# Moving part of the weight quantisation from the attention stage into the V projection, with smaller reduction pieces and a third x3w buffer

## The chip, the cores and the metric

The kernel runs on the 8 cores of one Trainium2 chip. Each core takes one of the 8 batch rows, 2048 tokens of width 1024, and runs the same program; no core talks to another. The metric is the device time of the slowest core in microseconds, as the median over runs.

## The reference, cut to what matters

```python
x = x + _layernorm(_L0_attn_ref(_layernorm(x), wq, bq, wk, bk, wv, bv, wo, bo))
x = x + _layernorm(_L0_ffn_ref(_layernorm(x), w1, conv_w, conv_b, w2))

def _L0_attn_ref(...):        # 16 heads of 64, blocks of 128 queries
    ...
    scores = jnp.einsum('bhnqd,bhnkd->bhnqk', qb, kb) / float(np.sqrt(D))
    scores = jnp.where(band, scores, -jnp.inf)      # each block sees itself and its two neighbours
    ...

def weight_quant(w):
    scale = 1.0 / jnp.clip(jnp.mean(jnp.abs(w)), 1e-05)
    return jnp.clip(jnp.round(w * scale), -1, 1) / scale

def _L0_ffn_ref(x, w1, conv_w, conv_b, w2):
    ...
    h = bit_linear(x, w1)                 # activations to 8 bits, weights to -1, 0, 1
    h = depthwise_conv1d(h.transpose(0, 2, 1), conv_w, conv_b)
    h = h.transpose(0, 2, 1)
    h = jax.nn.silu(h)
    return bit_linear(h, w2)
```

Both feed-forward weights (1024 x 4096, 16.8 MB each as float32) must be read twice: once for the mean of their absolute values, and once to be rounded to -1, 0 or 1 with the scale that comes from that mean.

## The kernel before

The program is a list of blocks. Inside a block each engine (SP, TensorE or PE, VectorE or DVE, ScalarE or ACT, GpSimd or POOL) replays its own list in the order in which the Python code called `p.op`; it waits on semaphores where the call says so. Nothing reorders an engine's list. At the end of a block each engine waits for its own semaphores, its DMAs among them, and all engines meet at a barrier.

- **b1** (to 107 us): layer norm of x and its transposition into `B1`.
- **b2** (107 to 393 us): the projections. GpSimd's queue loads `wq` and `wk` (16 DMAs, float32 in memory, written as bf16, 256 KB each on arrival), later `wv` (8 DMAs, issued when the Q projection is through). SP's queue loads the feed-forward weights in pieces into two buffers `wstage` (L324), and DVE sums their absolute values (L326): 16 pieces of `w1t`, 128 x 2048 (1 MB), then 32 pieces of `w2t`, 128 x 1024 (512 KB). A piece is loaded when the piece before last has been summed. PE meanwhile does the Q and K projections (L339). When the last sum is there, a few small steps give the scales `swc` (L359 to L376, the last one named `n6`); then DVE takes the maxima of Q and K (L387, L390), a chain of small steps gives the softmax bound, with one small DMA on SP's queue (L407), and the V projection follows: 32 groups of 8 matmuls (L439) in four PSUM slots, each moved out by DVE (L445).
- **b3** (393 to 887 us): the attention, 16 heads of 18 key blocks, 288 iterations, 256 of them with work on all engines: scores on PE (L582), exponential on ACT (L589), mask on POOL (L595), three matmuls of the result (L553), reciprocal and scaling on DVE (L561, L563). After each iteration `tern_gen` is asked for two steps of the weight quantisation. It works through 64 jobs of 128 x 1024 in pairs, 10 steps a pair: two loads (L488), two `tern_u` (L494, called n1 here), two more passes in place (L501, n2), two last passes (L510, n3) and two stores (L518). With a and b for the two slots of a pair, the order is La Lb n1a n1b n2a n2b n3a n3b Sa Sb. There are two slots, so the load of a slot waits until the store of the pair before has landed. 32 pairs take 160 iterations; the last 128 iterations have none. Jobs 0 to 31 are `w1t` (stored as int8 in `w1i`), jobs 32 to 63 are `w2t` (bf16, `w2b`).
- **b4** (887 to 1209 us): output projection, layer norms, 8-bit quantisation of the activations into `x3tsp`.
- **b5** (1209 us to the end): the feed-forward part in 8 stages of 256 tokens. Stage s does, chunk by chunk (32 chunks), the convolution of s (L927) and the first matmul of s + 2 (L898, on `w1h` from GpSimd's queue, L880, and `x3w` from SP's queue, L870), and then the second matmul of s - 1 (L967, `w2b` by SP, L952). `x3w` has two buffers. Its load stands at the head of a stage in SP's list, behind the two output stores (L1005) of the second matmul before:

```python
    for s in range(NS):
        s2 = s + 2
        if s2 <= NS:
            emit_x3ld(s2)
        for hcx in range(HCH):
            emit_conv_chunk(s, hcx)
```

Of the kernel before, what the change touches and what calls it, by code (L numbers as in the profile page):

```python
# [6 lines left out]
F32 = mybir.dt.float32  # L7
BF16 = mybir.dt.bfloat16
# [11 lines left out]
D = 1024  # L20
# [84 lines left out]
def build_nc():  # L105
# [68 lines left out]
    bks = alloc("bks", [128, NC], F32)  # L174
    bvrow = alloc("bvrow", [1, D], F32, side="right")
    borow = alloc("borow", [1, D], F32, side="right")
    bvB = alloc("bvB", [128, D], F32, side="right")
    boB = alloc("boB", [128, D], F32, side="right")
# [117 lines left out]
    free("xin_0", "xin_1", "x1b_0", "x1b_1", "ptr_0", "ptr_1", "pbc_0", "pbc_1")  # L296

    wsb = [[alloc(f"wsb{s}_{c}", [128, D], BF16) for c in range(NC)] for s in range(2)]
    wstage = [alloc(f"wstage_{i}", [128, 2048], F32) for i in range(2)]
# [3 lines left out]
    p = Plan()  # L303
    wq_ld = [0] * NC
# [54 lines left out]
    n1 = p.op("tensor", lambda e: e.matmul(pms[0:1, 0:48], onescol[:, :], wsum[:, 0:48],  # L359
                                           start=True, stop=True),  # L360
              waits=[(sV, red_done[-1])], inc=sT)
    n2 = p.op("scalar", lambda e: e.copy(mrow[0:1, 0:48], pms[0:1, 0:48]),
              waits=[(sT, n1)], inc=sS)
    p.op("vector", lambda e: e.reduce_sum(mtot[0:1, 0:1], mrow[0:1, 0:16], axis=AXX),
         waits=[(sS, n2)])
    nr2 = p.op("vector", lambda e: e.reduce_sum(mtot[0:1, 1:2], mrow[0:1, 16:48], axis=AXX))
# [61 lines left out]
    for t in range(NT):  # L428
        for ofs in range(2):
# [8 lines left out]
            for ic in range(NC):  # L438
# [11 lines left out]
                waits=[(sT, last)], inc=sV)  # L450

# [16 lines left out]
    tern_jobs = []  # L468
    for ch in range(NC):
        for q in range(4):  # L470
            tern_jobs.append((dw1t[ch * 128:(ch + 1) * 128, q * 1024:(q + 1) * 1024],
                              dw1i[q, :, ch * 1024:(ch + 1) * 1024], 0))
    for ch in range(HCH):
        tern_jobs.append((dw2t[ch * 128:(ch + 1) * 128, :],
                          dw2b[:, ch * 1024:(ch + 1) * 1024], 1))
    tstate = {"sp": [0, 0]}

    def tern_steps():
        for i0 in range(0, len(tern_jobs), 2):
            picks = [k for k in (i0, i0 + 1) if k < len(tern_jobs)]  # L480
            lds, n1s, n2s, obufs = {}, {}, {}, {}
            for k in picks:
                srcA, dst, wi = tern_jobs[k]
                slot = k % 2
                wl = [(sV, n6)]
                if tstate["sp"][slot]:
                    wl.append((sSp[slot], tstate["sp"][slot]))
                lds[k] = p.op("sync", lambda e, srcA=srcA, slot=slot: e.dma_start(  # L488
                    out=wstage3[slot][:, :], in_=srcA), waits=wl, inc=sW[slot], amt=16)
                yield  # L490
            for k in picks:
                wi = tern_jobs[k][2]
                slot = k % 2
                n1s[k] = p.op("vector", lambda e, slot=slot, wi=wi: e.tensor_scalar(  # L494
                    out=tern_u16[slot][:, :], in0=wstage3[slot][:, :],
                    scalar1=swc[:, wi:wi + 1], scalar2=RC, op0=ALU.mult, op1=ALU.add),
                    waits=[(sW[slot], lds[k])])
                yield
            for k in picks:
                slot = k % 2  # L500
                n2s[k] = p.op("vector", lambda e, slot=slot: e.tensor_scalar(  # L501
                    out=wstage3[slot][:, :], in0=tern_u16[slot][:, :],
                    scalar1=RD, scalar2=1.0, op0=ALU.subtract, op1=ALU.min),
                    waits=[(sV, n1s[k])])
                yield
            for k in picks:
                slot = k % 2
                wi = tern_jobs[k][2]
                obufs[k] = tern8[slot] if wi == 0 else tern2b[slot]
                n2s[k] = p.op("vector", lambda e, slot=slot, obuf=obufs[k]: e.tensor_scalar(  # L510
                    out=obuf[:, :], in0=wstage3[slot][:, :],
                    scalar1=-1.0, scalar2=None, op0=ALU.max),
                    waits=[(sV, n2s[k])], inc=sV)
                yield
            for k in picks:
                slot = k % 2
                dst = tern_jobs[k][1]
                tstate["sp"][slot] = p.op("sync", lambda e, dst=dst, slot=slot, obuf=obufs[k]: e.dma_start(  # L518
                    out=dst, in_=obuf[:, :]), waits=[(sV, n2s[k])], inc=sSp[slot], amt=16)
                yield  # L520

    tern_gen = tern_steps()

    def win(j):
        q0 = (j - 1) * 128
        q1 = (j + 2) * 128
        c0 = max(0, -q0)
# [488 lines left out]
    for s in range(NS):  # L1016
        s2 = s + 2
        if s2 <= NS:
            emit_x3ld(s2)
# [165 lines left out]
```

How the kernel before makes its waits and increments, by code:

```python
    def replay(self, eng, e, hwm):  # L60
        for w, emit, inc, amt in self.items[eng]:
            for s, v in w:
                if hwm[eng].get(s.name, 0) < v:
                    e.wait_ge(s.h, v)
                    hwm[eng][s.name] = v
            ins = emit(e)
            if inc is not None:
                ins.then_inc(inc.h, amt)
        for s in self.incs[eng].values():
            if hwm[eng].get(s.name, 0) < s.n:
                e.wait_ge(s.h, s.n)
                hwm[eng][s.name] = s.n
```

## Time and profile before

| | us |
|---|---|
| median of 2 runs | 2260.27 (2257.5 and 2263.03) |
| the profiled execution | 2256.83 |
| span of its slowest core, core 1 | 2255.3 |
| spans of the other cores | 2236.7 to 2248.0 |
| busy in that span: PE, DVE, ACT, POOL | 1216.7, 975.6, 619.8, 321.6 |

No engine is busy for much more than half of the span, so the time is made of stages with different limits, one behind the other. All rows below are of core 1 of the profiled execution; times in a timeline run from the start of its span.

### The profile page before, as it was taken

How to read it: one execution, taken by the hardware profiler on the slowest of the kernel's cores; microseconds unless marked ns; L12 is line 12 of the kernel's file. 1: busy time of each engine (PE TensorE's matmuls, PEld its weight loads, DVE VectorE, ACT ScalarE, POOL GpSimd, SP SyncE). 2: the span in 40 equal slices, each digit the busy share in tenths (PEclk: the TensorE clock that was granted, in tenths of full speed). 3: DMA queues.
4: the chain of work that ended last, by engine and by line, in shares of the span. 5: the costliest groups of instructions: out<-in, count | busy, mean ns of one | idle time of the engine just before them, and what ended most of it. 6: DMA issues, size and time to landing. Idle time of an engine off the chain costs nothing. (4 is left out here: it accounts for less than half of the span.)

```text
span 2255.3 us, 24795 instructions; the slowest of 8 cores (2236.7 to 2255.3 us)
## 1 busy us (share of the span) xinstructions
PE 1216.7 (54%) x6594; PEld 627.6 (28%) x6594; DVE 975.6 (43%) x2260; ACT 619.8 (27%) x1648; POOL 321.6 (14%) x383
## 2 busy tenths in 40 slices
PE   2349519232333475444441767757676757655455
PEld 1124204111111132111110555525252525242122
DVE  3434473454555543555551004535252525262624
ACT  2314200221222354122220345515151615141200
POOL 0000000333333487000000111101010101000000
PEclk9999759555555555666665888889898989858588
DMA  2398600333344202222225785646464646454044
GB/s 70 100 247 222 195 28 1 112 99 111 126 137 139 99 1 48 41 56 59 54 59 116 177 224 132 150 179 157 173 163 158 178 167 170 141 149 144 33 134 174
DMA packets 155324, 277.63 MB, mean 123 GB/s; under 512 B 27827, under 2 KB 114100, under 8 KB 144822
## 3 DMA queue, kind: packets, MB, share of 16 engines
q1 hardware_dynamic: 72966, 184.68, 25.6%
q0 software_dynamic: 82224, 91.37, 18.2%
q8 instruction: 59, 0.97, 0.2%
q14 instruction: 75, 0.61, 0.1%
HBM read 220.57 MB, written 29.36 MB: 111 GB/s over the span
## 5 line engine op out<-in xcount | busy, mean ns | idle before, releaser
L898 PE MATMUL pA<-x3w,w1h 128*128 128x256 bf16 (+1 forms) x2304 | 289.2, 273 | 96.8 <-DMA w1h<-w1i 75.5
L595 POOL TENSOR_TENSOR expm<-expraw,sb_mask 128x384 bf16<-128x384 bf16 (+1 forms) x256 | 231.2, 918 | 450.0 <-ACT expraw L589 380.1
L967 PE MATMUL pM<-w2b,H2q 128*128 128x512 bf16 x1024 | 250.8, 404 | 67.6 <-DMA w2b<-w2b 44.1
L898 PEld LDWEIGHTS pA<-x3w,w1h 128*128 128x128 bf16 x2304 | 218.8, 103 | 147.0 <-issue 107.3
L553 PE MATMUL pod<-VA,expm 128*128 128x65 bf16 x768 | 103.3, 228 | 289.4 <-DVE B L563 155.5
L1031 DVE TENSOR_REDUCE apar<-H 128x256 f32<-128x2048 f32 x32 | 116.7, 3650 | 313.7 <-ACT H L933 313.7
L589 ACT ACTIVATE expraw<-psc,negC 128x384 bf16<-128x384 f32 (+1 forms) x256 | 145.0, 568 | 344.0 <-PE psc L582 321.2
L927 PE MATMUL pC<-Ab,diag 128*128 128x256 bf16 x768 | 149.4, 311 | 137.9 <-DVE tland L1101 83.4
L909 ACT ACTIVATE Ab<-pA,mwc 128x256 bf16<-128x256 f32 (+1 forms) x288 | 129.6, 450 | 147.0 <-PE pA L898 141.7
L880 POOL DMA_DIRECT2D w1h<-w1i x72 | 63.0, 875 | 733.8 <-PE pA L898 448.2
L553 PEld LDWEIGHTS pod<-VA,expm 128*128 128x128 bf16 x768 | 58.1, 107 | 388.7 <-issue 387.4
L967 PEld LDWEIGHTS pM<-w2b,H2q 128*128 128x128 bf16 x1024 | 101.6, 103 | 217.8 <-issue 121.5
L985 DVE BATCH_NORM_STATS2 stat<-out 128x6 f32<-128x512 f32 x16 | 11.0, 690 | 313.2 <-ACT out L981 313.2
L933 ACT ACTIVATE H<-pC,cbs 128x256 f32<-128x256 f32 x256 | 120.5, 471 | 60.5 <-PE pC L927 59.2
L339 PE MATMUL pq<-B,wsb 128*128 128x512 bf16 x512 | 112.5, 383 | 34.6 <-DMA wsb<-wq 34.6
L326 DVE TENSOR_REDUCE wsum<-wstage 128x1 f32<-128x1024 f32 (+1 forms) x48 | 75.5, 1575 | 111.9 <-DMA wstage<-w2t 58.1
L582 PE MATMUL psc<-QT,KT 64*128 64x384 bf16 (+1 forms) x256 | 123.0, 481 | 1.5 <-PEq L83 1.3
L494 DVE TENSOR_SCALAR tern_u<-wstage,swc 128x1024 int16<-128x1024 f32 x64 | 50.9, 797 | 168.5 <-DMA wstage<-w1t 91.7
L927 PEld LDWEIGHTS pC<-Ab,diag 128*128 128x128 bf16 x768 | 65.1, 104 | 200.7 <-issue 191.0
L981 ACT ACTIVATE out<-pM,sc2b 128x512 f32<-128x512 f32 x32 | 20.1, 679 | 305.8 <-PE pM L967 305.8
L682 PE MATMUL po<-wo,B 128*128 128x512 bf16 x256 | 90.3, 529 | 23.5 <-DMA wo<-wo 14.3
L1101 DVE TENSOR_TENSOR tland<-H,sxB 128x256 f32<-128x256 f32 x256 | 96.9, 419 | 4.4 <-ACT sxB L1089 3.2
(134 smaller groups left out, 1304.1 us busy)
## 6 DMA issues: line engine op xcount, KB each, us to landing
w1h<-w1i POOLq DMA_DIRECT2D x72, 1024.0 KB, 5.7
w2b<-w2b SPq DMA_DIRECT2D x64, 1024.0 KB, 5.2
wstage<-w2t SPq DMA_DIRECT2D x64, 512.0 KB, 4.1
wstage<-w1t SPq DMA_DIRECT2D x16, 1024.0 KB, 8.3
wstage<-w1t SPq DMA_DIRECT2D x32, 512.0 KB, 5.2
xin<-x SPq DMA_DIRECT2D x16, 512.0 KB, 3.7
w2b<-tern2b SPq DMA_DIRECT2D x32, 256.0 KB, 2.0
xre<-x SPq DMA_DIRECT2D x16, 512.0 KB, 5.8
```

What stands on the lines that cost most here:

```text
L339: last = p.op("tensor", lambda e, oc=oc, st=st, ic=ic, slot=slot, wset=wset: e.matmul(pq[slot][:, :], wsb[wset][ic][:, oc * 128:(oc + 1) * ...
L553: last_use = p.op("tensor", lambda e, qb=qb, j=j, h=h, sl=sl, wc=wc, first=first, lastc=lastc: e.matmul(pod[qb % 4][:, 0:65], expm[sl][:, ...
L582: nmm = p.op("tensor", lambda e, hc=hc, hr=hr, j=j, sl=sl, q0r=q0r, q1r=q1r, c0=c0, c1=c1: e.matmul(psc[sl][:, c0:c1], KT[hc][hr:hr + 64, ...
L589: psc_ev[sl] = p.op("scalar", lambda e, h=h, sl=sl, c0=c0, c1=c1: e.activation(out=expraw[sl][:, c0:c1], in_=psc[sl][:, c0:c1], func=AF.Ex ...
L595: mask_done[sl] = p.op("gpsimd", lambda e, sl=sl, c0=c0, c1=c1: e.tensor_tensor(expm[sl][:, c0:c1], expraw[sl][:, c0:c1], mask01[:, c0:c1] ...
L898: last = p.op("tensor", lambda e, j=j, hs2=hs2, d=d, slotp=slotp, mv=mv, width=width: e.matmul(pA[slotp][:, 0:width], w1h[j % 2][:, d * 51 ...
L909: pa_ev[slotp] = p.op("scalar", lambda e, s2=s2, hcx=hcx, slotp=slotp, width=width: e.activation(out=ab(s2, hcx)[:, 0:width], in_=pA[slotp ...
L927: last = p.op("tensor", lambda e, s=s, hcx=hcx, k=k: e.matmul(pC[:, 0:256], dg(k, hcx), ab(s, hcx)[:, k:k + 256], start=(k == 0), stop=(k ...
L933: silu_d[s][hcx] = p.op("scalar", lambda e, s=s, hcx=hcx: e.activation(out=H2[:, hcx * 256:(hcx + 1) * 256], in_=pC[:, 0:256], func=AF.Sil ...
L967: last = p.op("tensor", lambda e, sm=sm, hcx=hcx, tsl=tsl, ofs=ofs, b=b, qq=qq, slot=slot: e.matmul(pM[slot][:, :], H2q[sm % 2][:, hcx * 2 ...
L1031: apar_d[s][g3] = p.op("vector", lambda e, g3=g3: e.reduce_max(apar[:, g3 * 256:(g3 + 1) * 256], H2.ap().rearrange("p (c n) -> p n c", c=H ...
L1101: ntl[i] = p.op("vector", lambda e, hcx=hcx, i=i: e.tensor_tensor(tland[i][:, :], H2[:, hcx * 256:(hcx + 1) * 256], sxB[:, :], ALU.mult), ...
```

## The change

Four things change.

1. The quantisation buffers and `tern_steps` are set up before b2, and the V projection asks for six steps after each of its 32 groups. So 192 of the 320 steps, 19 pairs and the two loads of the 20th, stand in b2; the other 128 are drawn in b3 as before, two per iteration, over its first 64 iterations.
2. The sums over `w1t` use pieces of 128 x 1024 (512 KB), 32 of them in place of 16, and `wstage` is half as large. The small steps behind them (64 columns for 48) follow.
3. `x3w` has three buffers, the first three loads are issued ahead of the first chunk, and each later one is issued one stage earlier. A load also waits for the load before last.
4. `bvrow` and `borow` are allocated last on their side and freed after b1.

```diff
+    free("bvrow", "borow")
+
+    wstage3 = [alloc(f"wstage3_{i}", [128, 1024], F32) for i in range(2)]
...
-    wstage = [alloc(f"wstage_{i}", [128, 2048], F32) for i in range(2)]
+    wstage = [alloc(f"wstage_{i}", [128, 1024], F32) for i in range(2)]
...
     for ch in range(NC):
-        for h2 in range(2):
-            piece_srcs.append((dw1t[ch * 128:(ch + 1) * 128, h2 * 2048:(h2 + 1) * 2048], 2048))
+        for h4 in range(4):
+            piece_srcs.append((dw1t[ch * 128:(ch + 1) * 128, h4 * 1024:(h4 + 1) * 1024], 1024))
...
                 op0=ALU.mult, op1=ALU.add),
                 waits=[(sT, last)], inc=sV)
+            for _ in range(6):
+                next(tern_gen, None)
...
-    x3w = [alloc(f"x3w_{i}", [128, 8 * 256], BF16) for i in range(2)]
+    x3w = [alloc(f"x3w_{i}", [128, 8 * 256], BF16) for i in range(3)]
...
-        wl = [(sT, a_mm[s2 - 2][HCH - 1])] if s2 >= 2 else []
+        wl = [(sT, a_mm[s2 - 3][HCH - 1])] if s2 >= 3 else []
+        if s2 >= 2:
+            wl.append((sX[s2 % 2], x3_ld[s2 - 2]))
...
+    emit_x3ld(0)
+    emit_x3ld(1)
+    emit_x3ld(2)
     for s2 in (0, 1):
-        emit_x3ld(s2)
...
     for s in range(NS):
         s2 = s + 2
-        if s2 <= NS:
-            emit_x3ld(s2)
+        if s + 3 <= NS:
+            emit_x3ld(s + 3)
```

On DVE, from the last steps of the softmax bound through the V projection to the first quantisation of b3, the list before is this (`VA` is the V result, `crow` the bound, `sb_mask` and `eC` belong to the first padded block of the attention):

```order
L405 COPY crow<-c2x 1x8 [waits sV]
L445 SCALAR_TENSOR_TENSOR VA<-pq,bvB 128x8x64 [waits sT] x32
L83 UNCONDITIONAL_BRANCH [waits sV]
L92 UNCONDITIONAL_BRANCH [waits barrier_Pool_Activation_PE_DVE_SP_release]
L603 TENSOR_SCALAR expm<-sb_mask,eC 128x128 [waits sS]
L494 TENSOR_SCALAR tern_u_0<-wstage_0,swc 128x1024 [waits sW0]
L494 TENSOR_SCALAR tern_u_1<-wstage_1,swc 128x1024 [waits sW1]
```

In the changed kernel the same place on DVE begins so (L509 is the old L445, L330, L337 and L346 are the old L494, L501 and L510):

```order
L509 SCALAR_TENSOR_TENSOR VA<-pq,bvB 128x8x64 [waits sT]
L330 TENSOR_SCALAR tern_u_0<-wstage_0,swc 128x1024 [waits sW0]
L330 TENSOR_SCALAR tern_u_1<-wstage_1,swc 128x1024 [waits sW1]
L337 TENSOR_SCALAR wstage_0<-tern_u_0 128x1024 [waits sV]
L337 TENSOR_SCALAR wstage_1<-tern_u_1 128x1024 [waits sV]
L509 SCALAR_TENSOR_TENSOR VA<-pq,bvB 128x8x64 [waits sT]
L346 TENSOR_SCALAR tern_0<-wstage_0 128x1024 [waits sV]
L346 TENSOR_SCALAR tern_1<-wstage_1 128x1024 [waits sV]
L509 SCALAR_TENSOR_TENSOR VA<-pq,bvB 128x8x64 [waits sT]
L330 TENSOR_SCALAR tern_u_0<-wstage_0,swc 128x1024 [waits sW0]
L330 TENSOR_SCALAR tern_u_1<-wstage_1,swc 128x1024 [waits sW1]
```

The 32 moves out of PSUM stood in one row; now one to seven instructions of the quantisation stand between two of them, and each `tern_u` waits for its load's semaphore with the moves behind it. The pattern repeats after three pairs and five moves.

On SP in b5, from the first stages on, the list before is this:

```order
L870 DMA x3w<-x3tsp 128x8x256 x2
L870 DMA x3w<-x3tsp 128x8x256 [waits sT] x2
L945 DMA x2re<-x2sp 128x1024 x2
L952 DMA w2b<-w2b 128x4096 x2
L952 DMA w2b<-w2b 128x4096 [waits sT] x6
L1005 DMA out<-x4b 128x1024 [waits sV] x2
L870 DMA x3w<-x3tsp 128x8x256
```

In the changed kernel it is this (L879, L954, L961 and L1014 are the old L870, L945, L952 and L1005):

```order
L879 DMA x3w<-x3tsp 128x8x256 x2
L879 DMA x3w<-x3tsp 128x8x256 [waits sX0]
L879 DMA x3w<-x3tsp 128x8x256 [waits sT,sX1]
L879 DMA x3w<-x3tsp 128x8x256 [waits sT,sX0]
L954 DMA x2re<-x2sp 128x1024 x2
L961 DMA w2b<-w2b 128x4096 x2
L961 DMA w2b<-w2b 128x4096 [waits sT] x6
L1014 DMA out<-x4b 128x1024 [waits sV] x2
L879 DMA x3w<-x3tsp 128x8x256 [waits sX1]
```

Five loads stand ahead of the first second matmul in place of four, so the load behind the output stores is now the one for the stage after.

## Rows read from the trace of the kernel before

**Rows 1.** Table of six stretches: busy us (instructions) per engine, granted PE clock, DMA

```profile
core 1: us, PE busy (x) PEld busy (x) DVE busy (x) ACT busy (x) POOL busy (x), PEclk, DMA share, GB/s
107.70:165.00 57.30, 23.37 (x100) 10.23 (x101) 18.29 (x8) 9.31 (x13) 8.44 (x16) 1.00 0.99 242
165.00:194.40 29.40, 29.40 (x138) 13.31 (x137) 18.29 (x9) 11.73 (x18) 0.00 (x0) 1.00 0.77 262
...
291.50:331.50 40.00, 1.07 (x6) 0.72 (x6) 36.52 (x26) 0.50 (x3) 0.00 (x0) 0.50 0.00 1
334.00:392.70 58.70, 58.54 (x258) 26.11 (x258) 21.51 (x31) 0.38 (x2) 0.00 (x0) 0.95 0.00 1
393.70:775.20 381.50, 115.30 (x573) 46.31 (x574) 196.22 (x491) 82.82 (x145) 134.60 (x144) 0.51 0.38 121
775.20:887.00 111.80, 87.19 (x452) 37.51 (x451) 55.01 (x246) 63.47 (x112) 96.55 (x112) 0.50 0.01 5
```

**Rows 2.** Timeline of DVE in b2, start and duration in us: the sums

```profile
192.11 3.41 DVE L326 TENSOR_REDUCE wsum<-wstage 128x1 f32<-128x2048 f32 x2 [1.77 <-DMA wstage<-w1t]
...
225.44 1.22 DVE L326 TENSOR_REDUCE wsum<-wstage 128x1 f32<-128x1024 f32 x1 [1.61 <-DMA wstage<-w2t]
...
290.24 1.22 DVE L326 TENSOR_REDUCE wsum<-wstage 128x1 f32<-128x1024 f32 x1 [1.69 <-DMA wstage<-w2t]
```

**Rows 3.** DMA issues in b2: count, KB each, median us to landing

```profile
wstage<-w1t SPq DMA_DIRECT2D x16, 1024.0 KB, 8.3
wstage<-w2t SPq DMA_DIRECT2D x32, 512.0 KB, 4.1
```

**Rows 4.** Line 445, moves of V: ns min/median/max, first and last start

```profile
L445 DVE SCALAR_TENSOR_TENSOR VA<-pq,bvB x32: 693/694/695, 338.3 to 392.7; 128x512 bf16<-128x512 f32 x32
```

**Rows 5.** Timeline of SP's queue in b2 and b3

```profile
331.02 0.76 SPq L407 DMA_DIRECT2D crow<-c2x  x1
...
503.43 1.64 SPq L518 DMA_DIRECT2D w1i<-tern  x2
505.26 2.83 SPq L488 DMA_DIRECT2D wstage<-w1t  x2
...
625.26 2.19 SPq L488 DMA_DIRECT2D wstage<-w2t  x2
```

**Rows 6.** Timeline of DVE in b3, line 494 (n1): first pair, and a later one

```profile
398.57 2.80 DVE L494 TENSOR_SCALAR tern_u<-wstage,swc 128x1024 int16<-128x1024 f32 x2 [4.46 <-DMA wstage<-w1t]
...
512.16 0.75 DVE L494 TENSOR_SCALAR tern_u<-wstage,swc 128x1024 int16<-128x1024 f32 x1 [6.10 <-DMA wstage<-w1t]
```

**Rows 7.** Groups of instructions of DVE: busy us, mean ns, idle before

```profile
L561 DVE RECIPROCAL rodc<-pod 128x1 f32<-128x1 f32 x256 | 41.3, 161 | 43.4 <-PE pod L553 43.2
...
L563 DVE TENSOR_SCALAR B<-pod,rodc 128x64 bf16<-128x64 f32 x256 | 72.6, 284 | 29.9 <-DVE rodc L561 3.2
```

**Rows 8.** Line 510 (n3), `w1t` jobs: ns min/median/max

```profile
L510 DVE TENSOR_SCALAR tern<-wstage x32: 679/684/1402, 403.2 to 589.5; 128x1024 int8<-128x1024 f32 x32
```

**Rows 9.** DMA issues from 393 to 590 us, and from 591 to 776 us

```profile
wstage<-w1t SPq DMA_DIRECT2D x32, 512.0 KB, 5.2
...
wstage<-w2t SPq DMA_DIRECT2D x32, 512.0 KB, 4.2
```

**Rows 10.** Tile `wstage` over the span: us from issue to landing

```profile
DMA to landing us min/median/max: 3.5/4.5/12.1
```

**Rows 11.** Tile `x3w`: who waited for its loads (us, times)

```profile
  PE pA L898: 20.5, 5
```

**Rows 12.** Timeline of PE, then POOL, at the head of a stage of b5

```profile
1512.73 0.80 PE L927 MATMUL pC<-Ab,diag 128*128 128x256 bf16 x3 [12.14 <-DVE tland L1101]
1518.06 1.86 PE L898 MATMUL pA<-x3w,w1h 128*128 128x256 bf16 x8 [4.54 <-DMA x3w<-x3tsp]
...
1532.55 1.03 PE L898 MATMUL pA<-x3w,w1h 128*128 128x256 bf16 x8 [1.77 <-DMA w1h<-w1i]
...
1525.04 0.87 POOL L880 DMA_DIRECT2D w1h<-w1i  x1 [73.39 <-PE pC L927]
```

More of the change, by code:

```diff
@@ new lines, in build_nc, with tern_steps @@
+    for ch in range(HCH):
+        tern_jobs.append((dw2t[ch * 128:(ch + 1) * 128, :],
+                          dw2b[:, ch * 1024:(ch + 1) * 1024], 1))
+    tstate = {"sp": [0, 0]}
+    def tern_steps():
+        for i0 in range(0, len(tern_jobs), 2):
+            picks = [k for k in (i0, i0 + 1) if k < len(tern_jobs)]
+            lds, n1s, n2s, obufs = {}, {}, {}, {}
+            for k in picks:
+                srcA, dst, wi = tern_jobs[k]
+                slot = k % 2
+                wl = [(sV, n6)]
+                if tstate["sp"][slot]:
+                    wl.append((sSp[slot], tstate["sp"][slot]))
+                lds[k] = PB["p"].op("sync", lambda e, srcA=srcA, slot=slot: e.dma_start(
+                    out=wstage3[slot][:, :], in_=srcA), waits=wl, inc=sW[slot], amt=16)
+                yield
+            for k in picks:
+                wi = tern_jobs[k][2]
+                slot = k % 2
+                n1s[k] = PB["p"].op("vector", lambda e, slot=slot, wi=wi: e.tensor_scalar(
+                    out=tern_u16[slot][:, :], in0=wstage3[slot][:, :],
+                    scalar1=swc[:, wi:wi + 1], scalar2=RC, op0=ALU.mult, op1=ALU.add),
+                    waits=[(sW[slot], lds[k])])
+                yield
+            for k in picks:
+                slot = k % 2
+                n2s[k] = PB["p"].op("vector", lambda e, slot=slot: e.tensor_scalar(
+                    out=wstage3[slot][:, :], in0=tern_u16[slot][:, :],
+                    scalar1=RD, scalar2=1.0, op0=ALU.subtract, op1=ALU.min),
+                    waits=[(sV, n1s[k])])
+                yield
+            for k in picks:
+                slot = k % 2
+                wi = tern_jobs[k][2]
+                obufs[k] = tern8[slot] if wi == 0 else tern2b[slot]
+                n2s[k] = PB["p"].op("vector", lambda e, slot=slot, obuf=obufs[k]: e.tensor_scalar(
+                    out=obuf[:, :], in0=wstage3[slot][:, :],
+                    scalar1=-1.0, scalar2=None, op0=ALU.max),
+                    waits=[(sV, n2s[k])], inc=sV)
+                yield
+            for k in picks:
+                slot = k % 2
+                dst = tern_jobs[k][1]
+                tstate["sp"][slot] = PB["p"].op("sync", lambda e, dst=dst, slot=slot, obuf=obufs[k]: e.dma_start(
+                    out=dst, in_=obuf[:, :]), waits=[(sV, n2s[k])], inc=sSp[slot], amt=16)
+                yield
@@ L303, in build_nc @@
     p = Plan()
+    PB["p"] = p
     wq_ld = [0] * NC
@@ L467, in build_nc @@
     p = Plan()
[L468 to L520, printed above, removed]
```

38 lines of the change are left out of this document (22 added, 16 removed).

## The prediction, made before the changed kernel ran

> **What bounds the kernel now.** I read the table of stretches first, because the kernel is a chain of blocks with a barrier after each: what a change is worth is read inside its block. The reader is to see in [rows 1] that no block is bound by a busy engine where the change works. In the sums (107.7 to 194.4 us) the DMA is full for the first 57 us and DVE, which has to wait for each piece, is busy for a third to two thirds. From 291.5 to 331.5 only DVE works. In the V projection PE is full: 58.54 of 58.70 us, DMA and POOL idle. In the first part of the attention, 381.5 us long, nothing is busy for more than half; in the second, without quantisation, 111.8 us, POOL is busy for 96.55. Then I read the timelines for what each of these waits for.
>
> The sums are a chain of load, sum, load. Between 225.44 and 290.24 us stand 24 intervals of 2.70 us for a piece of 512 KB [rows 2], with two slots: landing 4.1 [rows 3] and a sum of 1.22 make 5.3 a pair. PE's K projection is over long before the last sum, so this chain, not PE, ends there; every microsecond on it moves the V projection.
>
> The first part of the attention is a chain of the same kind. Stores are issued at 503.43, the next loads at 505.26 when the first store has landed, and n1a starts at 512.16 [rows 5, 6]: 8.7 us from store to n1a, of which DVE sits idle for 6.10. What is behind n1 in DVE's list (the moves out of the attention's PSUM) waits too, and so PE, ACT and POOL. From the first n1a (398.57) to that of the 20th pair (loads issued at 625.26, plus about 5) are 231.7 us for 19 pairs, 12.2 each.
>
> **The change part by part.** The sum is made against the profiled execution, 2256.8 us (span 2255.3 and 1.5 around it), which is 3.4 below the median of the two runs.
>
> *Quantisation in the V projection.* The loads of pair 1 can be issued when SP has passed the small DMA at 331.02 [rows 5], and have landed when the first V move ends (338.3 + 0.7 = 339.0) [rows 4]. From there DVE's list is the chain of pairs, with 32 moves of 0.69 in it. Five moves fall on three pairs, and by the order two of the five stand between n1a and the last n3a; the other three lie in the wait for loads and are free. So 0.46 us a pair on the chain, where the attention had two pairs of L561 and L563, 2 x (0.161 + 0.284) = 0.89 [rows 7]: 0.43 less. POOL does nothing in the V projection [rows 1], while in the attention an n3 takes up to 1402 ns against a median of 684 [rows 8]; I count 0.2 less for that. A pair takes 12.2 - 0.6 = 11.6. Nineteen pairs: 220.4, so the 20th pair's loads land at 559.4 and the attention starts at 561 in place of 393.7: +167.3. PE's 58.7 us now lie inside this and cost nothing more; if PE drops to the lower of its clock levels (0.50, 1.2 GHz, as it has at 0.51 in the attention [rows 1]), a group of 8 matmuls takes 3.7 us and one is wanted every 7: covered, as long as the pair chain is that slow.
>
> The attention loses what those 19 pairs took, 393.7 to 630.3: -236.6. The rest of the quantisation goes on as before. But 96 iterations ran beside those pairs and must now run by themselves. The stretch without quantisation gives 111.8/128 = 0.873 us each [rows 1], near POOL's own limit (96.55/111.8 busy): 96 x 0.873 = +83.8. Net: 167.3 - 236.6 + 83.8 = **+15**. The iterations were the cover of the quantisation; in the V projection there are only 58.7 us of other work to lay beside 220 us of chain, against 96 x 0.873 = 84 in the attention. Bounds: with loads landing in 4.2 (the `w2t` loads [rows 9]) rather than 5.2 a pair gets 1.0 shorter, 19 less, -4; with the shortest landing seen, 3.5 [rows 10], 1.7 shorter, -17; with no saving at all against the attention's 12.2, +26. I take +15, since 16 of the 19 pairs are `w1t`, which landed in 5.2 with an equally idle DMA.
>
> *Smaller pieces.* Sixteen pieces of 1 MB took from 107.7 to 194.3, 86.6 us, 16 `wq` and `wk` loads among them. In pieces of 512 KB the quiet rate is 32 x 2.70 = 86.4 already. What loads on the other queue add is seen behind it: from the first `w2t` sum (194.3) to the eighth (225.44) are 7 intervals in 31.1 us where 18.9 would be quiet, 12.2 for 8 `wv` loads; twice as many give 24. So 110.8, **+24**. Low end: only the quiet rest changes, 7 MB behind 165 us, 14 x 2.70 = 37.8 for 29.3 now: +9. High end: `w1t` in these pieces lands 1.0 later than `w2t` [rows 9], half of that per piece with two slots: +16, so +40. I take +24, nearest to the measured rows of the same size. K projection and Q loads don't bind.
>
> By the Trainium skill, DMA: Bandwidth & Descriptors, section "Anatomy of one DMA", a DMA takes about 2.0 us plus its bytes over 436 GB/s. That gives 3.2 us for 512 KB; with the sum of 1.22 a piece would take 2.2 us, and 32 quiet ones 71, so the pieces would cost 8 with the 24 of contention. The trace has 4.1 for that landing and 2.70 a piece [rows 2, 3], and the measurement decides.
>
> *Third `x3w` buffer.* PE waits five times for `x3w`, 20.5 us together [rows 11]: the load stands behind the output stores, the convolution starts at 1512.73 and the first matmul only at 1518.06 [rows 12]. One stage earlier, these waits go. What is late next: the third `w1h` piece of the stage. Its load goes out at 1525.04 today and its matmul waits 1.77 us, at 1532.55 [rows 12]. If A starts 4.5 earlier this load is issued earlier too, but into the `x3w`, `x2re` and two `w2b` loads that go out with the stage, some 3 MB. I give back 1 us in each of five stages: **-16**. Bounds -20.5 (nothing given back) and -8 (half lost, and the last stage's). The extra load at the start of b5 waits for the first to land and replaces a later one: 0. The order of the right-side buffers and the small steps: 0.
>
> Sum: 2256.8 + 15 + 24 - 16 = **2280**, 1% above its own time. Two per cent, 45 us, is about what a measurement of this kernel can tell from no change.
>
> **The rivals.**
> - *The pieces cost nothing that matters.* Two slots of 512 KB may leave the other queue more of the DMA, which then is through sooner; total traffic is the same and the DMA share is 0.99. Low end, +9: 2265. Against it: the `wv` stretch, where small pieces suffered. The page of the Trainium skill named above would give about this time, too, 2264, from its formula.
> - *The pieces are bound by slow `w1t` landings:* +40, 2296. For it: 5.2 against 4.2. Against it: the 4.2 and 5.2 come from a block with another rhythm.
> - *The quiet DMA shortens the V chain (the case on the other side, faster than before).* Nothing but the pair chain uses the DMA there, and POOL is idle [rows 1]. If a load lands in 3.5 in place of 5.2, a pair takes 9.9, the first term is -17, and with +9 for the pieces the time is 2257 - 17 + 9 - 16 = 2233. With +24 it decides at a pair of 10.4 us; below that the kernel gets faster. Against it: the attention's DMA share is 0.38, hardly busy either, and it had 5.2.
> - *The quantisation hides under V as DVE work alone.* If the loads ran ahead, V would last 32 x 0.69 + 19 x 4.2 = 102 us, +43 in place of +167: 2156. Against it: two slots and a load that waits for its slot's store; the change adds no slot. The order shows that load behind `sSp0`. It would need a wait that isn't one.
>
> **How the numbers follow.** Forecast, 2280 (2270 to 2290 on its own): 0.47. Pieces cheap, 2265: 0.20. Pieces slow, 2296: 0.17. V chain short, 2233: 0.13. Hidden, 2156: 0.03. The range 2250 to 2304 leaves out the hidden case, most of the short chain and the upper edge of the slow pieces. Slower by over 2% (above 2305) needs slow pieces together with 12.2 a pair: 0.10. Faster by over 2% (below 2215): the hidden case, 0.03. Within: 0.87.
>
> **What would show it.** The last sum at 315 rather than 291. In b2, n1 of successive pairs 11.6 us apart with DVE idle for some 5 to 6 us before n1a, PE at a low share and a low clock, the block's end near 585. The attention 340 us long, 64 iterations of it with quantisation, the rest at 0.87 us. No wait for `x3w` in b5 but a `w1h` wait of 2 to 4 us about eight chunks into a stage. The prediction is wrong if pairs in V are under 10.4 us or over 12.5, if the sums end before 300 or after 331, or if the stretch without quantisation doesn't keep 0.87.

## The result and the profile after

The changed kernel takes 2284.93 us as a median (2276.68 to 2296.22, 11 runs) beside 2260.08 (2253.21 to 2263.31, 10 runs) for the kernel before: a ratio of 1.0116 with a 95% interval of 1.0093 to 1.014. The forecast was 2280, within 2250 to 2304, and "within 2%" was the likeliest case. So the total came out; the terms behind it less so, and they are what the runs were spent on. Each experiment below stands beside the kernel before as measured in the same series, whose median was 2260, 2264 or 2269 us.

The profiled execution took 2280.29 us, and two cores share the end:

```profile
core 1: 2277.9 us, clock 0.728
core 5: 2278.8 us, clock 0.732
```

Before, core 1 stood alone at 2255.3 with the others up to 2248.0. I read core 1 in both kernels, and means over the 8 cores where cores differ.

The same table of stretches as [rows 1], for core 1 of the changed kernel (the `w1t` sums beside the `wq` and `wk` loads; part of them beside the `wv` loads; the `w2t` sums; the small steps; V; the attention with quantisation; the attention without):

```profile
core 1: us, PE busy (x) PEld busy (x) DVE busy (x) ACT busy (x) POOL busy (x), PEclk, DMA share, GB/s
107.70:165.00 57.30, 31.35 (x135) 13.78 (x136) 14.64 (x12) 12.28 (x17) 8.43 (x16) 1.00 0.88 194
165.00:200.00 35.00, 35.00 (x164) 15.84 (x162) 13.42 (x11) 13.74 (x20) 4.23 (x8) 1.00 0.63 171
...
235.00:323.40 88.40, 11.61 (x54) 5.10 (x52) 38.99 (x32) 5.12 (x8) 0.00 (x0) 0.59 0.62 183
323.40:362.00 38.60, 1.12 (x6) 0.72 (x6) 35.95 (x23) 0.36 (x2) 0.00 (x0) 0.50 0.00 0
370.30:563.30 193.00, 84.97 (x248) 29.30 (x246) 91.57 (x144) 0.00 (x0) 0.00 (x0) 0.69 0.39 125
572.10:710.60 138.50, 46.02 (x227) 18.30 (x227) 77.85 (x191) 34.02 (x59) 54.68 (x58) 0.50 0.41 137
710.60:910.50 199.90, 153.91 (x798) 66.08 (x798) 97.99 (x433) 112.27 (x198) 171.50 (x199) 0.50 0.01 4
```

The V projection, 58.7 us of full PE before, now takes 193 us from its first to its last move. PE is busy for 84.97 of them and DVE for 91.57: nothing is busy for more than half. POOL has nothing to do in it. In the last stretch POOL is at 171.50 of 199.90, as it was at 96.55 of 111.8. The 57.3 us at the head, whose DMA was full before (share 0.99, 242 GB/s), now move 194 GB/s.

DVE's timeline in b2 gives the ends of the `w1t` and of the `w2t` sums, and the n1a of the first, the fourth and the 19th pair, which is the last in V, and of the 20th, in the attention:

```profile
235.05 1.22 DVE L390 TENSOR_REDUCE wsum<-wstage 128x1 f32<-128x1024 f32 x1 [1.48 <-DMA wstage<-w2t]
...
322.23 1.22 DVE L390 TENSOR_REDUCE wsum<-wstage 128x1 f32<-128x1024 f32 x1 [1.48 <-DMA wstage<-w2t]
370.33 0.70 DVE L509 SCALAR_TENSOR_TENSOR VA<-pq,bvB 128x512 bf16<-128x512 f32 x1 [7.05 <-PE pq L503]
370.94 1.41 DVE L330 TENSOR_SCALAR tern_u<-wstage,swc 128x1024 int16<-128x1024 f32 x2
...
401.86 0.75 DVE L330 TENSOR_SCALAR tern_u<-wstage,swc 128x1024 int16<-128x1024 f32 x1 [4.72 <-DMA wstage<-w1t]
...
560.17 0.75 DVE L330 TENSOR_SCALAR tern_u<-wstage,swc 128x1024 int16<-128x1024 f32 x1 [5.17 <-DMA wstage<-w2t]
572.26 1.41 DVE L330 TENSOR_SCALAR tern_u<-wstage,swc 128x1024 int16<-128x1024 f32 x2
```

SP's queue beside it, one whole turn of the chain:

```profile
396.01 0.93 SPq L354 DMA_DIRECT2D w1i<-tern  x2
397.85 0.92 SPq L324 DMA_DIRECT2D wstage<-w1t  x2
```

Read one turn from the two views together: stores out at 396.01, loads out at 397.85 when the first store has landed (1.84), n1a at 401.86 (4.01 after the loads; DVE idle for 4.72 of the time before it). Before, the same three points stood at 503.43, 505.26 and 512.16 [rows 5, 6]: the same 1.83, but 6.90 from the loads to n1a. From the n1a of the first pair to that of the 19th it is (560.17 - 370.94)/18 = 10.51 us a pair. The moves did not become slower: 680/684/696 ns (shortest, median, longest) over all 32, beside 693/694/695 [rows 4].

How the stages compare, mean of the 8 cores in us, from the first or last starts of marking instructions on each core. "Sums end at" is the start of the last sum, "V" runs from the first V move to the first instruction of the attention on DVE, "b5" from the first issue of an `x3w` load to the end. The rows below the first two are the experiments of the next section, listed here once.

| | sums end at | V | attention | b4 | b5 |
|---|---|---|---|---|---|
| before | 291 | 55 | 483 | 324 | 1043 |
| after | 320 | 206 | 340 | 324 | 1030 |
| only_pieces | 323 | 55 | 480 | 324 | 1045 |
| only_x3w | 294 | 61 | 481 | 325 | 1032 |
| no_v_steps | 321 | 55 | 479 | 324 | 1029 |
| four_slots | 267 | 61 | 482 | 326 | 1056 |
| spread | 293 | 55 | 403 | 326 | 1049 |
| after_spread | 319 | 202 | 280 | 325 | 1042 |
| ahead | 295 | 55 | 363 | 326 | 1051 |
| ahead_spread | 293 | 55 | 327 | 325 | 1052 |
| v2_ahead | 265 | 59 | 314 | 326 | 1042 |
| v0_ahead | 262 | 55 | 328 | 326 | 1029 |
| v6_ahead | 261 | 107 | 280 | 325 | 1028 |

So the time went here: sums +29, V +150, attention -143, b5 -13, together +24 with the decimals that the table leaves out, which is the distance of the two executions (23.5). On core 1 alone the same four are +32, +146, -155 and -1. b5 varies by 10 to 27 us between the cores of one execution (17 before, 20 after), so a difference of a few microseconds in it is not read from one core.

### The profile page after: what moved, and what is told of

Its sections match the earlier page's. It is cut to its first block and busy times, and to the rows that moved or that the text cites. A ratio compares the mean times of both kernels' runs of the same rounds, so it can differ in the third digit from the quotient of the medians.

```text
span 2278.8 us, 24936 instructions; the slowest of 8 cores (2248.7 to 2278.8 us)
## 1 busy us (share of the span) xinstructions
PE 1241.0 (54%) x6594; PEld 632.3 (28%) x6594; DVE 974.7 (43%) x2276; ACT 619.9 (27%) x1648; POOL 316.6 (14%) x383
## 5 line engine op out<-in xcount | busy, mean ns | idle before, releaser
L907 PE MATMUL pA<-x3w,w1h 128*128 128x256 bf16 (+1 forms) x2304 | 289.1, 273 | 80.2 <-DMA w1h<-w1i 77.7
L602 POOL TENSOR_TENSOR expm<-expraw,sb_mask 128x384 bf16<-128x384 bf16 (+1 forms) x256 | 226.1, 899 | 504.6 <-ACT expraw L596 457.3
L560 PE MATMUL pod<-VA,expm 128*128 128x65 bf16 x768 | 97.2, 225 | 139.4 <-DVE B L570 49.7
L503 PE MATMUL pq<-wsb,B 128*128 128x512 bf16 x256 | 88.0, 519 | 98.1 <-DVE VA L509 98.1
L390 DVE TENSOR_REDUCE wsum<-wstage 128x1 f32<-128x1024 f32 x64 | 78.1, 1220 | 140.7 <-DMA wstage<-w1t 89.5
L330 DVE TENSOR_SCALAR tern_u<-wstage,swc 128x1024 int16<-128x1024 f32 x64 | 49.2, 773 | 172.0 <-DMA wstage<-w1t 99.7
```

The source lines that it names most:

```text
L560: last_use = p.op("tensor", lambda e, qb=qb, j=j, h=h, sl=sl, wc=wc, first=first, lastc=lastc: e.matmul(pod[qb % 4][:, 0:65], expm[sl][:, ...
L602: mask_done[sl] = p.op("gpsimd", lambda e, sl=sl, c0=c0, c1=c1: e.tensor_tensor(expm[sl][:, c0:c1], expraw[sl][:, c0:c1], mask01[:, c0:c1] ...
L907: last = p.op("tensor", lambda e, j=j, hs2=hs2, d=d, slotp=slotp, mv=mv, width=width: e.matmul(pA[slotp][:, 0:width], w1h[j % 2][:, d * 51 ...
```

## The experiments

**The parts by themselves.** `only_pieces` is the kernel before with part 2 of the change alone, `only_x3w` the same with part 3 alone. `no_v_steps` is the changed kernel with all 320 steps left to the attention, so it has parts 2 to 4 without the move:

```diff
-            for _ in range(6):
+            for _ in range(0):
                 next(tern_gen, None)
```

> The kernel before with only the sums over w1t cut into 32 pieces of 512 KB (two slots). Theory (round trip): two small pieces in flight don't fill the DMA; in the traces the last sum moved from 290 to 320 us on the mean of the cores, so this kernel alone is 29 us slower than before (about 2289), the last sum at 320, everything behind it unchanged. Rival (the other queue gets what the pieces leave): the sums lose only the quiet part, about +9, and the rest of the 29 comes from something else in the change. In numbers: 2282 to 2296 for the theory, 2265 to 2273 for the rival.

Measured: 2294.14 beside 2264.27, ratio 1.0118 (1.0088 to 1.0149), +27 us. The sums of core 1, then its loads of `w1t` in this part (KB, us from issue to landing):

```profile
L326 DVE TENSOR_REDUCE wsum<-wstage x64: 1219/1220/1221, 115.2 to 325.5; 128x1 f32<-128x1024 f32 x64
```

```profile
wstage<-w1t SPq DMA_DIRECT2D x32, 512.0 KB, 5.5
```

The last sum starts at 325.5 in place of 290.24, and nothing behind it moves but in scatter (V 55, attention 480). The smaller pieces alone cost about what the whole change costs. Half the bytes per slot means half the bytes in flight: a load of 512 KB lands in 5.5 us here where 1 MB took 8.3 [rows 3]. The Trainium skill, DMA: Bandwidth & Descriptors, section "Anatomy of one DMA", gives a fixed cost plus bytes for DMAs that GpSimd issues, while these are issued by SP; an estimate by that sum is 3.2 us for this landing. With eight cores reading, the trace has 5.5, and 4.1 to 5.2 where the queue beside it is quiet [rows 3, 9]. The measurement decides.

> The kernel before with only the third x3w buffer and the loads one stage earlier. Theory: the five waits (20.5 us) go and part comes back as w1h waits; the traces show b5 shorter by 13 us on the mean of the cores, so 2247 (2240 to 2252). Rival 1: all of it stays, 2240. Rival 2: b5's shortening is scatter between executions (b5 of one core differs by up to 17 us from another's in one trace) and this kernel is within 4 us of before.

Measured: 2251.73, ratio 0.9942 (0.9919 to 0.9965), -13 us. In core 1 of this kernel no wait for `x3w` is left in b5; PE waits for `w1h` instead:

```profile
  DMA w1h<-w1i: 81.3, 20
```

Before it was 75.5 us in 24 waits, so of the 20.5 us [rows 11] some 6 come back as `w1h` waits.

> The changed kernel with no quantisation steps in the V projection: all 320 steps are drawn in the attention as before, with the new buffers, small pieces and third x3w buffer left. Theory: the move is nearly a wash. V gets about 150 us longer and the attention 143 shorter by the traces, so without the move the time is 7 us (0 to 12) below the changed kernel's 2285, about 2278. Rival (the move is what makes the change slow): 20 us or more below, 2265. Rival (the move gains): above 2290.

Measured: 2277.57, ratio 1.005 (1.0032 to 1.0067). The change as a whole is at 1.0116, so the move is worth 0.0066, about +15 us; the two intervals together give 6 to 24. By stages it is V 55.2 to 205.6 and attention 479.3 to 339.6, +11 together. The forecast of +15 lies within what the times allow and somewhat above what the stages give. PE has the V projection at full speed again, and the attention is 480 us long as before:

```profile
core 1: us, PE busy (x) PEld busy (x) DVE busy (x) ACT busy (x) POOL busy (x), PEclk, DMA share, GB/s
370.00:425.00 55.00, 55.00 (x245) 24.43 (x244) 20.76 (x30) 0.17 (x1) 0.00 (x0) 0.95 0.00 1
425.00:905.00 480.00, 203.34 (x1026) 83.77 (x1025) 249.45 (x728) 145.62 (x256) 228.95 (x254) 0.51 0.30 97
```

Pieces and `x3w` by themselves multiply to 1.0118 x 0.9942 = 1.0059, against 1.005 (1.0032 to 1.0067) for `no_v_steps`, which has both: no sign that these two act on each other. For the move there is no such test, since its price is itself a difference. The move by itself on the kernel before wasn't tried: its buffers take 18 KB of each partition in b2, of which the halved `wstage` gives back 8 and the freed `bvrow` and `borow` another 8, and whether it would fit without them no run shows.

**Bytes in flight in the sums.** If two small pieces in flight are the trouble, four should cure it. `four_slots` is the kernel before with 512 KB pieces in four slots, the same memory as two of 1 MB:

```diff
-    sW = [Sem(nc, "sW0"), Sem(nc, "sW1")]
+    sW = [Sem(nc, f"sW{i}") for i in range(4)]
...
-    wstage = [alloc(f"wstage_{i}", [128, 2048], F32) for i in range(2)]
+    wstage = [alloc(f"wstage_{i}", [128, 1024], F32) for i in range(4)]
...
-        slot = idx % 2
-        wl = [(sV, red_done[idx - 2])] if idx >= 2 else []
+        slot = idx % 4
+        wl = [(sV, red_done[idx - 4])] if idx >= 4 else []
```

> The kernel before with 512 KB pieces in four slots (four semaphores), the same buffer memory as before. Theory (round trip): with four pieces in flight the chain is bound by the DMA's throughput; 33.6 MB of weights and 12.6 of wq, wk, wv at some 260 to 280 GB/s take 165 to 178 us, so the last sum stands at 272 to 285 and the time is 5 to 18 us below before, 2242 to 2255. Rival (small pieces or the 16 KB row stride of w1t are slow in themselves): the last sum stays above 305 us and the kernel at 2275 or more.

Measured: 2243.45, ratio 0.989 (0.9835 to 0.9946), -25 us. The sums end at 267 as a mean of the cores, earlier than the 272 to 285 that I expected:

```profile
L326 DVE TENSOR_REDUCE wsum<-wstage x64: 1219/1220/1221, 116.2 to 271.4; 128x1 f32<-128x1024 f32 x64
```

The same 64 pieces and the same 1.22 us of sum as in `only_pieces`, 54 us sooner. It is the number in flight and not the size of a piece that the small pieces took away. Single loads land later for it (`w1t` 10.4 us, `w2t` 5.8), but four are on their way.

**The cover.** My reading was that the iterations of the attention are the only work long enough to lie beside the chain of pairs. The kernel before spends two steps per iteration, so 160 iterations carry all of it at the chain's pace and 128 run bare. `spread` changes nothing but that rate, to 10 steps in 9 iterations:

```diff
-        for _ in range(2):
+        for _ in range(2 if idx % 9 == 0 else 1):
             next(tern_gen, None)
```

> The kernel before, with 10 quantisation steps drawn in 9 attention iterations (320 steps in 288) in place of 20 in 10 and none later. Nothing else changes. Theory (the pair chain of load, passes, store sets the pace, and attention iterations beside it are free): 32 pairs of 12.2 us cover all 288 iterations, the attention lasts 390 to 405 us in place of 483, and the time is about 2175 (2165 to 2190). Rival (an instruction that waits on DVE holds up the iterations, so each costs its own 0.87 us wherever it stands): attention still above 465 us, 2245 or more.

Measured: 2184.18 beside 2268.85, ratio 0.9644 (0.9603 to 0.9686), 3.56% or 81 us less. The attention goes from 483 to 403 us with the same instructions:

```profile
core 1: us, PE busy (x) PEld busy (x) DVE busy (x) ACT busy (x) POOL busy (x), PEclk, DMA share, GB/s
393.70:795.00 401.30, 209.22 (x1015) 84.00 (x1015) 246.78 (x722) 145.76 (x256) 241.63 (x254) 0.50 0.36 115
```

The first n1 stands at 398.1 and the last at 791.7 where 32 pairs used to end by 775. A pair has nine iterations beside it in place of five. From the first n1a to the 19th it takes 12.6 us on core 1, where it took 12.2 before, and as a mean of the cores 12.6 where it took 11.8: four more iterations, which bare cost 0.87 us each, lengthen a pair by about 1 us. The wait for loads has room for most of them.

`after_spread` asks the same of the changed kernel, whose remaining 128 steps become one in every second iteration.

> The changed kernel, its two slots and six steps per V group as they are, with the remaining 128 steps drawn one in every second attention iteration in place of two in each. Theory (the attention has far more cover than V, and it is free as long as the pairs come seldom): attention 275 to 300 us in place of 340, V unchanged at 206, the time 2220 to 2245, about 40 us above the kernel before with its steps spread (2184). Rival (spreading gains nothing once the first 192 steps are gone): attention above 330 us, 2275.

Measured: 2222.53, ratio 0.9826 (0.9765 to 0.9887): some 62 us under the changed kernel, whose median is from another series. V stays at 202; the attention falls from 340 to 280:

```profile
core 1: us, PE busy (x) PEld busy (x) DVE busy (x) ACT busy (x) POOL busy (x), PEclk, DMA share, GB/s
569.00:849.00 280.00, 196.53 (x1008) 83.77 (x1009) 193.08 (x609) 144.39 (x254) 242.89 (x253) 0.50 0.23 74
```

Yet V and attention together are 482 here and 458 in `spread`, which leaves V alone. With the attention's cover used in both, V and attention together are 24 us longer with the move.

**Loads that run ahead.** This is the rival "hidden" made real: what if the load doesn't wait for its slot's store? `ahead` is the kernel before with four load buffers. Loads go out a pair early, a load waits for the n3 four jobs before, and the wait for the store moves to the n3 that writes the store's buffer. To make room, `bvrow` and `borow` are freed after b1:

```diff
-                wl = [(sV, n6)]
-                if tstate["sp"][slot]:
-                    wl.append((sSp[slot], tstate["sp"][slot]))
+                wl = [(sV, n6)]
+                if k >= 4:
+                    wl.append((sV, n3s[k - 4]))
...
-                    waits=[(sV, n2s[k])], inc=sV)
+                    waits=wl, inc=sV)
```

> The kernel before with four load buffers for the quantisation: the loads of a pair are issued a pair ahead and wait for the last pass of the pair before last, not for a store; 20 steps in 10 iterations as before. Theory (the wait for the round trip is 5 of the 12 us of a pair): a pair takes 6.5 to 8 us, bound by DVE (4.3 us of passes and 5 iterations of 0.45), the part with quantisation 210 to 255 us in place of 369, the time 2105 to 2150. Rival (DVE and POOL hold each other up, or DMA bandwidth sets the pace): a pair stays above 10 us, 2200 or more.

Measured: 2149.26, ratio 0.948 (0.9439 to 0.9521), the attention 363 us. Its first part, all pairs with two steps per iteration, takes 250 us where it took 370, as means of the cores:

```profile
core 1: us, PE busy (x) PEld busy (x) DVE busy (x) ACT busy (x) POOL busy (x), PEclk, DMA share, GB/s
398.00:647.00 249.00, 113.20 (x569) 45.74 (x568) 227.61 (x486) 82.37 (x145) 170.39 (x144) 0.51 0.57 184
```

DVE is busy for 227.61 of 249 us: the part has changed from a chain of waits to an engine that is full. The DMA, at a share of 0.57 now against 0.38, was never the limit; the turn of store, load and landing was.

> Four load buffers and 10 steps in 9 iterations. Theory (each iteration is bound by the larger of POOL, 0.89 us, and DVE, 0.45 + 0.48, with some mutual blocking): attention 270 to 330 us, time 2040 to 2105, 20 us or more below the kernel with the four buffers alone. Rival (POOL's masks and DVE's passes exclude each other fully, 0.89 + 0.48 us an iteration): attention 390 us, no better than the four buffers alone with their stretch free of quantisation.

`ahead_spread` has both edits. Measured: 2111.87, ratio 0.9312 (0.9264 to 0.9359), 7 us above the range I gave. The attention is 327 us, inside the 270 to 330 expected, but at its edge: spreading gives 36 us here where it gave 80 alone. The two edits cure the same wait; what may set the 327 that remain stands in the last section.

**How much to put into V, once loads run ahead.** Three kernels on top of the changed one, with four buffers shared by sums and quantisation (loads ahead in both). They differ only in how many steps stand in V and at what rate the attention takes the rest: `v2_ahead` 2 per group and then 1 per iteration, `v0_ahead` none and 10 in 9 iterations, `v6_ahead` 6 and one in every second iteration.

```diff
-            for _ in range(6):
+            for _ in range(0):
                 next(tern_gen, None)
...
-        for _ in range(2):
+        for _ in range(2 if idx % 9 == 0 else 1):
             next(tern_gen, None)
```

(This is `v0_ahead`; the buffers are those of `four_slots` and `ahead`.)

> The changed kernel with four shared buffers for the sums and for the quantisation, loads a pair ahead, two quantisation steps per V group in place of six (64 steps), and one per attention iteration (256 steps). Theory: once no load is waited for, the V projection does cover a small share of the work (6.4 pairs x 4.3 us of DVE beside 58 us of PE): V is 55 to 65 us long, the sums end near 267 us, the attention lasts 270 to 320, the time 2020 to 2075. Rival (V's cover is lost even so, each pair lengthens V): V is 75 us or more.

> As v2_ahead (2068), but no quantisation step in the V projection and all 320 in the attention, 10 in 9 iterations. Theory: V covers a small share for nothing, so without it V is 55 us as before and the attention 327 in place of 314, the time about 9 us above v2_ahead, 2077 (2070 to 2086). Rival (V covers nothing, what it takes it adds): within 3 us of v2_ahead or below it.

> As v2_ahead, but with the changed kernel's six steps per V group (192 steps) and the other 128 in the attention, one in every second iteration. Theory (with the load wait gone a pair in V costs DVE's 4.3 us): V lasts 32 x 0.69 + 19 x 4.3 = 104 us and something for waits, 104 to 115, against 206 in the changed kernel; the attention 280 to 290; the time 2080 to 2095, still above v2_ahead, since V has only 58 us of PE to lay beside it. Rival (the store and load round trip still sets the pace in V): V 150 us or more, 2130.

Measured: 2068.41, ratio 0.9123 (0.9073 to 0.9173); 2057.63 (2054.52 to 2070.65), 0.9116 (0.906 to 0.9173); 2065.49, 0.9136 (0.9087 to 0.9185). In the order `v2_ahead`, `v0_ahead`, `v6_ahead`, all three beat the kernel before by some 195 to 200 us and the changed one by more, and their times can't be told from each other; the second and third came out 12 and 15 us below the ranges that I expected. For `v0_ahead` that is what the rival said: within 3 us of `v2_ahead` or below it. V and attention together, by stages, are 374, 383 and 387 us, so two steps per group do look 10 us better than none, as I had expected, and six are no better. But b5 was 1042 in the first and 1029 and 1028 in the others, from the same code, and that covers the ten. Whether V can hide a little of the quantisation for a gain stays open.

Where six steps stand in V and loads run ahead, V is 107 us, not 206. What DVE and PE wait for on core 1 (us, times, largest), there:

```profile
DVE tern_u L335 <- DMA wstage<-w1t: 8.8, 15, 1.4
PE pq L510 <- DVE VA L516: 26.9, 15, 4.3
```

DVE waits 8.8 us for loads of `w1t` there, where it waited 84.9 us in the V of the changed kernel, and PE now waits for DVE's moves behind the passes. The rival "hidden" gave 102 us for exactly this case.

## Why the prediction was right, and where it was not

**The total.** 2280 forecast, 2284.93 measured. The signed terms, in us:

| term | forecast | single parts, by ratio | stages, mean of 8 cores | core 1 |
|---|---|---|---|---|
| smaller pieces | +24 | +27 | +29 | +32 |
| move into V | +15 | +15 (6 to 24) | +7 | -9 |
| third `x3w` buffer | -16 | -13 | -13 | -1 |

By ratio each term is right in sign and within 3 us, the move with a wide interval. On core 1, which I had worked from, only the sum comes out; that was partly luck, and the part on the move shows where it came from.

**Smaller pieces: right mechanism, somewhat undersized.** "The last sum at 315 rather than 291": it stood at 322 on core 1 and 320 as a mean. What I added at 12.2 us per 8 `wv` loads was about right for the `wv` loads, but the order of the two queues changed. Before, `wq` and `wk` loads shared the DMA with `w1t` and the `wv` loads with `w2t`. Now all 24 fall beside `w1t`: the `wv` loads are issued in the stretch 165 to 200 (POOL busy 4.23 us with 8 instructions). The `w1t` part ends at 235 instead of 194 on core 1, 41 later, and the `w2t` part, now quiet, takes 322.2 - 235.0 = 87 instead of 96, 9 less. The price of contention was right: 24 loads beside `w1t` cost about 127 - 32 x 2.81 = 37 us, 1.6 each, where I had 12.2 for 8, 1.5 each. The step that was off is "in pieces of 512 KB the quiet rate is 32 x 2.70". The quiet `w2t` pieces of the changed kernel came (322.23 - 235.05)/31 = 2.81 apart; 0.11 more for each of 64 pieces is 7 us, which is most of the 8 between +24 and +32 on core 1. In the kernel before, the same 24 intervals that gave 2.70 on core 1 gave 2.70 to 2.89 on the eight cores. The rival of the "pieces bound by slow `w1t` landings" put 16 us on top of the forecast where 3 to 8 are there, and the rate of the `w2t` pieces accounts for as much. The rival "pieces cost nothing" is refuted by `only_pieces`.

**The move: the net was about right, both gross terms were too large.** I had 11.6 us a pair in V, as 12.2 less 0.63. It was 10.51 on core 1 and (574.43 - 370.31)/18 = 11.34 on core 5; core 4 stood at 11.14 and the others at 10.5 to 10.7. The attention began at 567 to 587 us, where the signs said 585:

```profile
370.31 1.41 DVE L330 TENSOR_SCALAR tern_u<-wstage,swc 128x1024 int16<-128x1024 f32 x2
...
574.43 0.75 DVE L330 TENSOR_SCALAR tern_u<-wstage,swc 128x1024 int16<-128x1024 f32 x1 [4.96 <-DMA wstage<-w2t]
```

Two terms of the 11.6 were mis-sized, and a turn taken apart shows both. The table has means over the first 15 turns in us, worked out from the start and landing times in the traces; 0.1 us between landing and n1a is left out.

| | n1a to store | store to next loads | load to landing | pair |
|---|---|---|---|---|
| before, core 1 | 5.21 | 1.94 | 5.09 | 12.36 |
| before, core 5 | 5.49 | 1.97 | 4.05 | 11.63 |
| no_v_steps (attention), core 1 | 5.39 | 1.92 | 4.18 | 11.59 |
| after (V), core 1 | 4.45 | 1.90 | 4.08 | 10.53 |
| after (V), core 5 | 4.28 | 2.11 | 4.94 | 11.42 |

The first is the landing. I took 12.2 a pair and 5.2 for a `w1t` load from core 1 as what the attention does. It is what cores 0 to 3 did in that one execution (medians of 5.0 to 5.2); cores 4 to 7 of the same execution had 4.4 to 4.6, and so had all eight cores of `no_v_steps`. In the changed kernel cores 4 and 5 are the late ones, with 5.2 and 5.3. Medians of before on core 5 from 393 to 590 us, of `no_v_steps` on core 1 in its attention, and of the changed kernel on cores 1 and 5 from 370 to 560 us:

```profile
wstage<-w1t SPq DMA_DIRECT2D x32, 512.0 KB, 4.5
wstage<-w1t SPq DMA_DIRECT2D x32, 512.0 KB, 4.5
wstage<-w1t SPq DMA_DIRECT2D x30, 512.0 KB, 4.5
wstage<-w1t SPq DMA_DIRECT2D x30, 512.0 KB, 5.3
```

So the landing does not belong to the stage: a quiet V has no shorter one than a quiet attention, and the 6.90 of the turn shown above was a late turn on a late core. In `after_spread`, whose V is the same code, no core is late and all eight stand at 10.4 to 10.6 us a pair. What makes some cores late in one execution stays open. The second term is the saving in V. Between n1a and the store, core 1 is 0.94 us shorter in V than in the attention of `no_v_steps`, where I had allowed 0.43 for the moves and 0.2 for n3. The n3 part was right in kind: over `w1t` it is 679/684/689 ns in V, and the 1402 of [rows 8] is gone. What the rest consists of, no run separates.

The rival "quiet DMA shortens the V chain" decides at 10.4 us a pair and was missed by 0.1 on most cores, but not by its mechanism: the pair was shorter on DVE's side, not in the landing. With like beside like (core 1 of `no_v_steps` and of the changed kernel) V is +146 and the attention -142, so +4; the -9 of core 1 in the table above is that plus a late before.

The attention gave back less than I took from it: -143 as a mean, not -152.8. I had taken 236.6 us for 19 pairs from core 1, and core 1 was the slowest of the cores in that part, 381 us against a mean of 370, for the landings just named. On core 1 itself the attention went from 494 to 338, -155, near what I had computed. So the step "the attention loses what those 19 pairs took" was mis-sized by being read on one core; the same 12.2 stood in the term for V, which is why the net suffered less than either. The step "96 x 0.873" held: from the start of the last n3 to the next block the bare stretch is 199.9/224 = 0.892 us an iteration, beside 0.888 before when it is measured in the same way.

What carried the forecast was the reasoning on cover, and it is now shown: `no_v_steps` gives the price of the move, `spread` and `after_spread` show that the bare iterations can lie beside the chain at little cost, and `ahead` that the chain is a wait and not work.

**PE's clock in V.** I had PE at the lower of its levels there. The granted clock is 0.69 as a mean over the block, between 0.50 (1.2 GHz) and 1.00 (2.4 GHz). No cost of it shows, since PE waits 98.1 us for the moves. The profile page's group, on core 5:

```profile
L503 PE MATMUL pq<-wsb,B 128*128 128x512 bf16 x256 | 88.0, 519 | 98.1 <-DVE VA L509 98.1
```

**Third `x3w` buffer: right, with some 2 to 6 us given back where 5 were forecast.** No wait for `x3w` stands in b5 any more. PE's waits for `w1h` rose from 75.3 to 77.7 us on core 5, and on core 1 from 75.5 to 81.9:

```profile
PE pA L907 <- DMA w1h<-w1i: 81.9, 23, 35.2
```

The head of a stage, to be set beside [rows 12]:

```profile
1538.67 0.80 PE L936 MATMUL pC<-Ab,diag 128*128 128x256 bf16 x3 [12.14 <-DVE tland L1112]
1539.26 1.91 PE L907 MATMUL pA<-x3w,w1h 128*128 128x256 bf16 x8
...
1554.46 1.03 PE L907 MATMUL pA<-x3w,w1h 128*128 128x256 bf16 x8 [1.20 <-DMA w1h<-w1i]
```

The first matmul follows the convolution after 0.6 us, where 5.3 lay between them. But the `w1h` wait that I named, 2 to 4 us some eight chunks on, is 1.20, shorter than the 1.77 before: what is given back lies elsewhere in the stage. That core 1 shows only -1 for the whole of b5 isn't explained by its waits (20.5 less 6.4 would be 14); it is inside the scatter of b5, and the mean of the cores and `only_x3w` both give 13.

## What to carry to other kernels

A chain of load, pass and store over two slots costs its turn-around wherever it stands; moving it only changes what lies beside it, so first count the work that covers it in the old place and in the new. Try the cheap cures before a move: the rate at which the steps are mixed in (3.6% for one line here) and loads that don't wait for the store of their slot (5.2%), and give the sums bytes in flight rather than smaller pieces. Take a duration that decides a term from several cores and, where there is one, from a second execution: the landing that I read on the slowest core, 5.2 us, was 4.4 to 4.6 on four of the others, and it was part of what made that core the slowest.

## What the runs showed of the hardware

- Two loads of 512 KB in flight with a sum of 1.22 us behind each give a piece every 2.7 to 2.9 us; four in flight end the same 64 pieces 54 us earlier (325.5 to 271.4) although a `w1t` load then takes 10.4 us to land instead of 5.5. The landing time of one load says little of the rate.
- The same 512 KB load of `w1t`, two at a time with no load on another queue, took a median of 4.4 to 4.6 us to land on most cores and 5.0 to 5.3 on some, which were cores 0 to 3 in the execution of the kernel before and cores 4 and 5 in that of the changed one.
- POOL's masks take longer where DVE's passes stand close together. In the bare stretch of the kernel before:

```profile
L595 POOL TENSOR_TENSOR expm<-expraw,sb_mask x112: 664/907/912, 776.6 to 884.9; 128x384 bf16<-128x384 bf16 x98, 128x256 bf16<-128x256 bf16 x14
```

and in the attention of `v0_ahead`, with passes all the way through and few waits:

```profile
L609 POOL TENSOR_TENSOR expm<-expraw,sb_mask x256: 662/1350/1468, 369.5 to 691.5; 128x384 bf16<-128x384 bf16 x112, 128x256 bf16<-128x256 bf16 x16
```

```profile
core 1: us, PE busy (x) PEld busy (x) DVE busy (x) ACT busy (x) POOL busy (x), PEclk, DMA share, GB/s
365.00:693.00 328.00, 199.20 (x1029) 85.23 (x1026) 266.12 (x733) 146.03 (x257) 294.69 (x256) 0.51 0.44 141
```

The median mask goes from 907 to 1350 ns, and POOL and DVE are busy for 294.69 and 266.12 of 328 us. `ahead_spread` and `v0_ahead`, which carry all of the quantisation in the attention, both stand at 327 to 328 us there. That this is a floor set by the two engines, each busy in part with waiting for the other, is a reading and not shown. Full exclusion, the rival of `ahead_spread`, would have given 390 us, so they do overlap in part. The Trainium skill, SBUF — State Buffer, section "SBUF: two separate sides", says that GpSimd and a VectorE operation in a fast mode take turns on one shared pair of ports, each holding it for a whole instruction. The n3 of up to 1402 ns against 684 in [rows 8], and masks of 1350, agree with that; no run here separates it from another cause, such as the DMA traffic beside them (141 GB/s against 5).
